# A fused attention and mixture-of-experts layer: expert work in steps of two 128-token tiles, x also passed turned, weights staged by single chunks

## The chip, the cores and the metric

The kernel runs on one core of one Trainium2 chip. Five engines have an instruction stream each: TensorE (PE; its weight loads are listed apart as PEld), VectorE (DVE), ScalarE (ACT), GpSimd (POOL) and SyncE (SP), which only issues DMA transfers. They meet at semaphores. A q behind an engine's name, as in PEldq or SPq, means the engine's own instruction queue: register work, waits and issues that keep no arithmetic unit busy. The metric is the device time of one execution in microseconds (us).

## The reference

8 batches of 512 tokens with 256 features go through linear attention with 16 heads and a gate, then through 16 experts, of which each token uses 4, and a shared expert.

```
q, k, v = heads(x @ Wq + bq), heads(x @ Wk + bk), heads(x @ Wv + bv)
q = elu(q) + 1;  k = elu(k) + 1
kv = einsum("bhsd,bhse->bhde", k, v);  attn = einsum("bhsd,bhde->bhse", q, kv)
x = layernorm(x + (sigmoid(x @ Wg + bg) * attn) @ Wo + bo)
scores = softmax(x @ gate_w.T)           # 16 experts in 4 groups
c = the scores of the 4 best experts inside the 2 best groups, else 0
a = silu(x @ w1[e]) * (x @ w3[e]);  y = sum_e c[:, e] * (a @ w2[e])
z = silu(x @ ws1) * (x @ ws3) @ ws2
out = layernorm(x + y + z)
```

Each expert has an inner width of 128, the shared one of 256.

## The kernel before

**Precision.** A large product is made of three 16-bit matmuls (`product`, lines 1147 to 1151): hi x hi, hi x lo, lo x hi. ScalarE makes the hi part of an operand (a copy to fp16), VectorE the lo part (the difference, bf16).

**Attention, 8 batches.** For batch b TensorE projects k and v of four token tiles, between them the output projection of batch b-1 (`project_out`), transposes x of batch b+1 (`transpose_x(x_in)`, line 1243), projects q, transposes the normalized x1 of batch b-1, projects the first half of the gate, sums k times v (`sum_kv`), projects the second half, counts and routes, and attends. x is loaded into `x_in`; its copy with the output bias is made on VectorE (`x_plus_bias`). VectorE's order in a batch: gate, routing of b-2, residual and norm statistics of b-1, lo parts of x, k, a weight split, q, lo parts of x1, kv, routing head. The reciprocal root of the norm is taken on GpSimd (`rstd_of`, four small operations), the normalization on ScalarE. The expert weights go to SBUF in nine stages of two chunks (an expert's w1, w3, w2 together are a chunk) and are split there (`split_hi`, `split_lo`). SyncE issues all loads in one hand-written order, with fills of zeros of 512 KB for rows of the sorted buffer that no token writes.

**Dispatch.** The batches form two waves of four. GpSimd scatters each token's x1 four times to a DRAM buffer sorted by expert (`expert_in`), 128 rows an instruction (line 440). Each expert has a region there. `plan_pairs` computes which expert and which row each pair has.

**Experts, 2 x 48 pairs.** A pair is 256 tokens of one expert: 16 tiles x 4 / 2 = 32 full pairs, and up to one partly filled for each of the 16 experts. For pair g:
- SyncE reads the row number from SBUF (`value_load`, line 327), waits for a free one of four token buffers, loads 256 rows (line 330) and stores the results of pair g-7 (line 334, `expert_out`).
- TensorE transposes the tokens of pair g+2 (`transpose_xs`), reads the number of the expert's weight chunk into a register (`chunk_of`, line 1345), makes four products of 256 columns (`up_pair`), and the down projection of pair g-2 (`down_pair`), six matmuls. Weight addresses hang on that register, so the queue computes them: two register instructions a product. `two_groups` is the body of a hardware loop over eight pairs; the first two of each turn read the chunk of pair g-2 again (line 1389).
- ScalarE: hi part of the transposed tokens, silu, results to SBUF, hi part of a. VectorE: lo part (1025), silu times h3 (line 1036), lo part of a (1044), and in some pairs a piece of the plan or, in wave 1, a `combine` of wave 0.

GpSimd gathers each token's four results (line 452) once a wave is stored, and VectorE adds them with their weights (1055).

**Tail.** The shared expert of batches 3 to 7, gathers and sums of wave 1, the final norms and stores.

The order of work is written out by hand on each engine; there is no scheduler.

## Time and profile before

| What | us |
|---|---|
| median of the runs (711.7 to 711.9) | 711.87 |
| the profiled execution | 707.36 |
| its span, first to last instruction | 705.5 |
| TensorE busy / VectorE / ScalarE / GpSimd | 527.1 / 427.4 / 300.1 / 290.1 |
| attention and first shared work, until the first token transposes | 266 |
| line 1036, first to last (96 pairs) | 273.8 to 588.8 |
| the rest | 117 |
| DMA: moved, mean rate | 118.6 MB, 168 GB/s |

The engines overlap, so the busy times are no sum. In the chain of work that ended last TensorE has 36% of the span, VectorE 19% and "issue" 15%: time in which an engine waited for nothing that the profile shows. SyncE's queue has 9%, and 6% is laid to another core or an unknown queue. The mean granted clock of TensorE is 0.916 of 2.4 GHz; it has only two levels, 2.4 and 1.2 GHz. A matmul's duration in the records is longer than its spacing, since matmuls are pipelined; the distance between two starts is what it costs. Of queue instructions the profile shows count, duration and the first and last start in a stretch.

### The profile page before, as it was taken

Reading aid. Unit: us, or ns where it says so; the run is one execution under the profiler, and the core shown is the slowest. Engines: PE = TensorE matmul, PEld = TensorE weight load, DVE = VectorE, ACT = ScalarE, POOL = GpSimd, SP = SyncE. Lnnn points to the kernel's source line nnn. Section 1 sums busy time; section 2 is a strip of 40 time slices with the busy share of each in tenths; the row PEclk is TensorE's granted clock in tenths of the full one; section 3 lists DMA queues with packets and bytes.
Section 4 is the critical chain, followed back from the end, with each engine's and each line's share of the span. In section 5 each row is a group of like instructions: output and inputs, shape, how many; then the busy total and the mean of one; then the engine's idle time right before and its main releaser. Section 6 shows DMA issues by size and latency. Waiting matters only on the chain.

```text
span 705.5 us, 13461 instructions
## 1 busy us (share of the span) xinstructions
PE 527.1 (75%) x3532; PEld 357.0 (51%) x3555; DVE 427.4 (61%) x1200; ACT 300.1 (43%) x659; POOL 290.1 (41%) x334
## 2 busy tenths in 40 slices
PE   1899887889897688789786688798888779665400
PEld 1355443555544357567574566576667566421300
DVE  2447783776864866666554444377757556652784
ACT  2536653436524343555454555356546445110100
POOL 1000126456446402454444200644446251777574
PEclk9999997899999899999999999899999989977755
DMA  7022428295451303767767766687787753333332
GB/s 202 13 75 76 156 90 284 82 304 209 177 185 68 103 18 106 239 204 230 232 228 259 238 223 216 180 235 233 211 261 231 223 181 134 105 120 89 94 114 99
DMA packets 64091, 118.63 MB, mean 168 GB/s; under 512 B 9760, under 2 KB 23088, under 8 KB 64048
## 3 DMA queue, kind: packets, MB, share of 16 engines
q1 hardware_dynamic: 51216, 84.55, 37.1%
q0 software_dynamic: 12288, 33.57, 15.1%
q8 instruction: 19, 0.31, 0.2%
q14 instruction: 24, 0.20, 0.1%
q10 hardware_dynamic: 544, 0.00, 0.0%
HBM read 55.17 MB, written 62.91 MB: 167 GB/s over the span
## 4 chain that ended last, share of the span: by engine, by line
PE 36%; DVE 19%; issue 15%; SPq 9%; another core or an unknown queue 6%; ACT 6%; DMA 5%; POOL 4%; ACTq 0%; DVEq 0%; POOLq 0%
PE t L1340 4%; PE h_even L1149 4%; PE h_even L1151 4%; PE h_odd L1149 3%; PE h_even L1150 3%; PE h_odd L1151 3%; PE h_odd L1150 3%; DVE x_all L1055 2%; SPq L327 2%; PE y L1186 2%; DMA kv<-expert_in 2%; SPq L330 1%; PE y L1373 1%; SPq L334 1%
## 5 line engine op out<-in xcount | busy, mean ns | idle before, releaser
L440 POOL DMA_INDIRECT expert_in<-x_all,slots x128 | 132.9, 1038 | 117.8 <-PE h_odd L1151 45.0
L452 POOL DMA_INDIRECT wa_stage<-expert_out,result_of x64 | 62.9, 983 | 35.3 <-issue 18.1
L1340 PE MATMUL t<-ident,kv 128*128 128x128 f32 x384 | 60.3, 280 | 19.4 <-DMA kv<-expert_in 15.0
L452 POOL DMA_INDIRECT q_fm<-expert_out,result_of x32 | 32.4, 1014 | 85.6 <-DMA expert_out<-q_exp 63.9
L426 POOL TENSOR_SCALAR neg_mean<-mv 128x4 f32<-128x4 f32 x16 | 4.6, 290 | 149.5 <-DVE mv L699 149.3
L1044 DVE TENSOR_TENSOR wa_lo<-bias_heads,wa_hi 128x256 bf16<-128x256 f32 x96 | 40.5, 422 | 41.3 <-ACT wa_hi L642 30.1
L1149 PE MATMUL h_even<-xsT_hi,we_hi 128*128 128x256 f16 x192 | 54.3, 283 | 10.7 <-issue 8.8
L1340 PEld LDWEIGHTS t<-ident,kv 128*128 128x128 f32 x384 | 45.3, 145 | 26.8 <-DMA kv<-expert_in 12.1
L1025 DVE TENSOR_TENSOR xsT_lo<-t,xsT_hi 128x512 bf16<-128x512 f32 x72 | 49.5, 688 | 11.6 <-ACT xsT_hi L617 5.9
L1150 PE MATMUL h_even<-xsT_lo,we_hi 128*128 128x256 bf16 x192 | 54.2, 282 | 2.5 <-issue 2.5
L1151 PE MATMUL h_even<-xsT_hi,we_lo 128*128 128x256 f16 x192 | 54.2, 282 | 1.4 <-issue 1.4
L617 ACT ACTIVATE xsT_hi<-t 128x512 f16<-128x512 f32 x72 | 42.0, 585 | 16.6 <-PE t L1340 12.8
L642 ACT ACTIVATE wa_hi<-bias_heads 128x256 f16<-128x256 f32 x96 | 39.7, 414 | 20.7 <-DVE bias_heads L1036 14.4
L1036 DVE TENSOR_TENSOR bias_heads<-h_odd,kv_heads 128x256 f32<-128x256 f32 x48 | 20.2, 420 | 41.8 <-ACT kv_heads L634 40.9
L1036 DVE TENSOR_TENSOR bias_heads<-h_even,kv_heads 128x256 f32<-128x256 f32 x48 | 20.1, 419 | 34.4 <-ACT kv_heads L634 30.9
L634 ACT ACTIVATE kv_heads<-h_odd 128x256 f32<-128x256 f32 x48 | 18.3, 381 | 52.8 <-remote 25.0
L1186 PE MATMUL y<-wo_sb,gated 128*128 128x256 f32 x128 | 33.3, 419 | 9.3 <-DVE gated L686 9.3
L452 POOL DMA_INDIRECT gate<-expert_out,result_of x32 | 30.5, 954 | 19.4 <-PE h_even L1151 10.0
L529 ACT ACTIVATE kv<-h_even 128x256 f32<-128x256 f32 x32 | 12.3, 386 | 58.3 <-PE h_even L1151 52.4
L634 ACT ACTIVATE kv_heads<-h_even 128x256 f32<-128x256 f32 x48 | 18.2, 380 | 43.8 <-PE h_even L1151 17.4
L1367 PE MATMUL y<-we_hi,wa_hi 128*128 x96 | 26.8, 279 | 12.6 <-issue 10.7
L624 ACT ACTIVATE k_exp<-y 128x512 f32<-128x512 f32 x48 | 28.7, 598 | 15.9 <-PE y L1373 14.3
(222 smaller groups left out, 1530.0 us busy)
## 6 DMA issues: line engine op xcount, KB each, us to landing
kv<-expert_in SPq DMA_DIRECT2D x96, 256.0 KB
expert_out<-k_exp SPq DMA_DIRECT2D x48, 256.0 KB
expert_out<-q_exp SPq DMA_DIRECT2D x48, 256.0 KB
expert_in<-wa_stage SPq DMA_DIRECT2D x16, 512.0 KB
expert_in<-wa_stage SPq DMA_DIRECT2D x32, 256.0 KB
stage<-in_L_ffn_w SPq DMA_DIRECT2D x48, 128.0 KB
x_in<-in_L_attn_x SPq DMA_DIRECT2D x8, 512.0 KB
out<-gated SPq DMA_DIRECT2D x8, 512.0 KB
```

The costliest lines, as they stand in the source:

```text
L440: pool.indirect_dma_start(xs_dram[b // WB], bass.IndirectOffsetOnAxis(ap=slots[:, b, t, j:j + 1], axis=0), x_all[:, b, t, :], None).then_i ...
L452: pool.indirect_dma_start(y_got[i][:, j, :], None, ys_dram[w], bass.IndirectOffsetOnAxis(ap=result_of[:, b, t, j:j + 1], axis=0)).then_inc ...
L617: act.activation(xsT_hi[r][:, :, :], t_bank[r % 2][:, :].rearrange("p (c n) -> p c n", c=KC), ACT.Copy).then_inc(xst_hi_ready, 1)
L642: act.activation(aT_hi[r % 2][:, :], a_pair, ACT.Copy).then_inc(at_hi_ready, 1)
L1025: dve.tensor_tensor(xsT_lo[r][:, :, :], t_bank[r % 2][:, :].rearrange("p (c n) -> p c n", c=KC), xsT_hi[r][:, :, :], ALU.subtract).then_in ...
L1036: dve.tensor_tensor(a_pair, h_banks[r % 2][0][:, 2 * P:], s_pair, ALU.mult).then_inc(pair_a_ready, 1)
L1044: dve.tensor_tensor(aT_lo[r % 2][:, :], a_pair, aT_hi[r % 2][:, :], ALU.subtract).then_inc(at_lo_ready, 1)
L1149: pe.matmul(dst, sta_hi, mov_hi, start=start, stop=False)
L1150: pe.matmul(dst, sta_hi, mov_lo, start=False, stop=False)
L1151: return pe.matmul(dst, sta_lo, mov_hi, start=False, stop=stop)
L1186: last = pe.matmul(y_bank[h][:, (t % 2) * D:(t % 2 + 1) * D], gated[:, c, t * P:(t + 1) * P], wo_sb[:, c, :], start=c == 0, stop=c == KC - 1)
L1340: last = pe.transpose(t_bank[r % 2][:, c * 2 * P + i * P:c * 2 * P + (i + 1) * P], xs[r][:, i, c * P:(c + 1) * P], ident[:, :])
```

## The change

**Steps of two tiles.** A region is cut in tiles of 128 tokens: 64 full ones and up to 16 partly filled, 80 a wave. A step takes tile p and tile p+40, in general of two experts. So there are 40 steps a wave instead of 48 pairs. SyncE reads two rows and issues two loads of 128 tokens. TensorE reads two chunk numbers and makes, in each half of the columns, four products of 128 columns; the down projection is one product for each tile. The transposes write their 128 columns with a step of two. Zero fills shrink to half.

```diff
-                row = sp.value_load(pair_row[0:1, NPAIR * w + p, :], min_val=0, max_val=SLOTS - PAIR)
+                rows = [sp.value_load(tile_row[0:1, h, NPAIR * w + p, :], min_val=0, max_val=SLOTS - P) for h in range(2)]
...
-                sp.dma_start(xs[r][:, :, :], rows_of(xs_dram[w], row)).then_inc(xs_loaded[r], 16)
+                for h in range(2):
+                    sp.dma_start(xs[r][h * P // 2:(h + 1) * P // 2, :, :],
+                                 rows_of(xs_dram[w], rows[h])).then_inc(xs_loaded[r], 16)
...
+            def chunks_of(g):
+                return [pe.value_load(tile_chunk[0:1, h, g, :], min_val=SHARED, max_val=NCH - 1) for h in range(2)]
...
+                for h, chunk in enumerate(chunks):
+                    tok = slice(h * P, (h + 1) * P)
+                    for k in range(2):
+                        for c in range(KC):
...
+                            last = product(h_banks[r % 2][0][:, k * PAIR + h * P:k * PAIR + (h + 1) * P],
+                                           we_hi[:, chunk, cols], we_lo[:, chunk, cols],
+                                           xsT_hi[r][:, c, tok], xsT_lo[r][:, c, tok], c == 0, c == KC - 1)
...
+                for h, chunk in enumerate(chunks):
+                    last = product(y_bank[r % 2][:, h * D:(h + 1) * D],
+                                   aT_hi[r % 2][:, h * P:(h + 1) * P], aT_lo[r % 2][:, h * P:(h + 1) * P],
+                                   we_hi[:, chunk, W13:], we_lo[:, chunk, W13:], True, True)
```

```order
L1340 MATMUL t<-ident,kv 128x128 x4
L1345 TENSOR_LOAD pair_chunk
L1345 ISA x2
L1149 ISA
L1149 MATMUL h_even<-xsT_hi,we_hi 128x256
L1150 MATMUL h_even<-xsT_lo,we_hi 128x256
L1151 REGISTER_ALU
L1151 MATMUL h_even<-xsT_hi,we_lo 128x256
```

and now:

```order
L1344 MATMUL t<-ident,kv 128x128 x4
L1348 ISA
L1348 TENSOR_LOAD tile_chunk
L1348 ISA x3
L1348 TENSOR_LOAD tile_chunk
L1348 ISA x2
L1165 ISA
L1165 MATMUL h_even<-xsT_hi,we_hi 128x128
L1166 MATMUL h_even<-xsT_lo,we_hi 128x128
L1167 REGISTER_ALU
L1167 MATMUL h_even<-xsT_hi,we_lo 128x128
```

The last five rows of each come four times in a row before, and eight times now, with half the columns. Then the down projection of the step two back: one ISA and one REGISTER_ALU before, two of each now. With the two or three instructions that wait, that is 17 register instructions a pair before and 31 a step now.

SyncE's queue in its first loop over wave 0, one load and one store. Before:

```order
L327 ISA
L327 TENSOR_LOAD pair_row
L327 ISA x2
L329 REGISTER_ALU
L330 ISA
L330 DMA kv<-expert_in 128x512
L333 REGISTER_ALU
L334 ISA
L334 DMA expert_out<-q_exp 128x512
```

and now:

```order
L331 TENSOR_LOAD tile_row
L331 ISA x3
L331 TENSOR_LOAD tile_row
L331 ISA x2
L333 REGISTER_ALU
L335 ISA
L335 DMA kv<-expert_in 64x512
L335 ISA
L335 DMA kv<-expert_in 64x512
L339 ISA
L340 ISA
L340 DMA expert_out<-k_exp 128x512
```

A second row number is read, and a second DMA issued, each of half the partitions.

**x turned.** The host passes x a second time with features outside; `load_xt` brings it to `x_in` as [128, 2, 512], and ScalarE and VectorE split it there. TensorE transposes x no more. x itself goes straight into `x_all`, where `x_plus_bias` adds the bias; x of batch 0 is issued behind the small loads and the first weight chunk. In TensorE's order the first half of the gate comes ahead of the transposes of x1, and the wait for the next batch's lo parts is at the batch's start.

```diff
-                if nxt:
-                    transpose_x(x_in, x_transposed)
...
                 project_features(b, 0, 2 * D, q_projected)
                 project_features(b, 1, 2 * D, q_projected)
-                if nxt:
-                    pe.wait_ge(xt_lo_ready, KC * (b + 2))
+                pe.wait_ge(q_exp_ready, KC * b + 1)
+                project_features(b, 0, 3 * D, g_projected)
...
                 if prev:
                     pe.wait_ge(x1_ready, b)
                     transpose_x(x_all[:, b - 1, :, :], x1_transposed)
-                pe.wait_ge(q_exp_ready, KC * b + 1)
-                project_features(b, 0, 3 * D, g_projected)
                 sum_kv(b)
```

**Weights by chunks.** Each of the 18 chunks is loaded, split and released alone, three a batch in batches 0 to 5: after the second k/v tile, between the gate's halves, and at the end (ScalarE); after k, after the lo parts of x1, and at the end (VectorE).

```diff
+            def load_chunk(c):
+                a1, a3, a2 = chunk_sources(c)
+                if c >= 2:
+                    sp.wait_ge(we_lo_ready, c - 1)
...
+            for b in range(1, 6):
+                next_x(b + 1)
+                load_chunk(3 * b + 1)
+                load_chunk(3 * b + 2)
+                if b > 1:
+                    for i in range(2 * (b - 2), 2 * (b - 1)):
+                        fill_spare(i)
+                if b < 5:
+                    load_chunk(3 * b + 3)
```

**Plan and norms.** `plan_tiles` has nine steps on rows of 80 tiles (eight on 48 pairs before) and for wave 0 stands behind the last residual instead of ahead of the shared expert's first product. `place_results` has a step more, for the two halves. Variance plus epsilon, and where it is used the negated mean, are computed on VectorE in `norm_moments`; GpSimd keeps the power and, but for the last five norms, the product. In wave 1 the final norms of batches 0 to 2 go from VectorE to ScalarE (`final_norm`, in a step each tile from step 17 on), and the combines are spread evenly over the 40 steps.

```diff
             def rstd_of(ln):
                 pool.wait_ge(mv_ready, ln + 1)
-                pool.tensor_scalar(neg_mean[:, :], mv[:, :, 0], -1.0, None, ALU.mult)
-                pool.tensor_tensor(var_eps[:, :], mv[:, :, 1], eps[:, :], ALU.add).then_inc(rstd_step, 1)
...
+                power = pool.tensor_tensor(rstd[:, :], var_eps[:, :], minus_half[:, :], ALU.pow)
```

## Rows read from the trace of the kernel before

**Rows 1.** Three stages: us, busy us and instructions of each engine, granted clock, DMA, GB/s
```profile
0.00:266.00 266.00, 214.23 (x1174) 123.08 (x1194) 168.75 (x538) 120.02 (x255) 90.79 (x114) 0.94 0.41 135
266.00:589.00 323.00, 262.20 (x2114) 207.68 (x2112) 191.56 (x492) 166.36 (x380) 127.34 (x136) 0.96 0.69 217
589.00:705.50 116.50, 50.71 (x248) 26.22 (x250) 67.12 (x172) 13.69 (x24) 71.96 (x84) 0.73 0.34 107
```
**Rows 2.** Line 1036, a pair's h3*silu on VectorE: durations (ns), first to last start (us)
```profile
L1036 DVE TENSOR_TENSOR bias_heads<-h_even,kv_heads x48: 402/420/426, 273.8 to 586.8; 128x256 f32<-128x256 f32 x48
L1036 DVE TENSOR_TENSOR bias_heads<-h_odd,kv_heads x48: 403/424/426, 275.8 to 588.8; 128x256 f32<-128x256 f32 x48
```
**Rows 3.** Who waited for whom, 266 to 589 us: total us, times, longest
```profile
PEld h_even L1149 <- issue: 19.8, 38, 1.3
...
PEld y L1367 <- issue: 18.4, 24, 1.3
...
PE t L1340 <- DMA kv<-expert_in: 15.0, 11, 3.8
...
PEld t L1340 <- DMA kv<-expert_in: 12.1, 7, 4.0
```
**Rows 4.** TensorE's own queue, lines 1345, 1149, 1151: count, durations (ns), starts
```profile
L1345 PEldq TENSOR_LOAD <-pair_chunk x5: 298/302/605, 466.5 to 476.0; - x5
...
L1345 PEldq TENSOR_LOAD <-pair_chunk x1: 302/302/302, 564.4 to 564.4; - x1
...
L1149 PEldq FUSED_REGOPS  x4: 46/46/46, 565.0 to 565.8; - x4
...
L1151 PEldq ALU_OP  x4: 32/32/32, 565.2 to 565.9; - x4
```
**Rows 5.** TensorE in order of time: start us, us, line, matmul
```profile
563.06 0.60 PE L1340 MATMUL t<-ident,kv 128*128 128x128 f32 x4
563.50 0.27 PE L1149 MATMUL h_even<-xsT_hi,we_hi 128*128 128x256 f16 x1
563.61 0.27 PE L1150 MATMUL h_even<-xsT_lo,we_hi 128*128 128x256 bf16 x1
...
565.46 0.60 PE L1340 MATMUL t<-ident,kv 128*128 128x128 f32 x4
```
**Rows 6.** SyncE's DMA issues in order of time, a fast and a slow stretch
```profile
562.65 0.35 SPq L330 DMA_DIRECT2D kv<-expert_in  x1
563.88 0.33 SPq L334 DMA_DIRECT2D expert_out<-k_exp  x1
...
338.60 0.73 SPq L330 DMA_DIRECT2D kv<-expert_in  x1
340.11 0.01 SPq L334 DMA_DIRECT2D expert_out<-q_exp  x1
342.38 0.71 SPq L330 DMA_DIRECT2D kv<-expert_in  x1
```
**Rows 7.** Who waited for whom, 0 to 266 us
```profile
ACT we_hi L516 <- DMA stage<-in_L_ffn_w: 31.8, 7, 7.4
...
DVE logits L730 <- remote: 19.8, 5, 8.9
...
PE t L1156 <- ACT x_all L510: 17.6, 7, 5.8
...
PEld t L1156 <- ACT x_all L510: 10.9, 2, 6.3
```
**Rows 8.** The start in order of time: last small load, x plus bias
```profile
6.63 0.42 SPq L281 DMA_DIRECT2D plan_sb<-in_plan_consts  x1
...
14.49 1.22 DVE L704 TENSOR_TENSOR x_all<-x_in,b_o 128x1024 f32<-128x1024 f32 x1 [6.29 <-DMA plan_sb<-in_plan_consts]
```
**Rows 9.** GpSimd in order of time, the last normalization
```profile
699.16 0.23 POOL L426 TENSOR_SCALAR neg_mean<-mv 128x4 f32<-128x4 f32 x1 [4.34 <-DVE mv L699]
...
700.74 0.20 POOL L431 TENSOR_TENSOR shift<-neg_mean,rstd 128x4 f32<-128x4 f32 x1
```

More of the change, by code:

```diff
@@ L17 @@
 P = 128
-PLAN_STEPS = 8
+PLAN_STEPS = 9
 LN_EPS = 1e-5
@@ L654, in _ @@
             group(1)
-            with act.Fori(1, all_groups // 2 - 1) as q2:
+            with act.Fori(1, GROUPS_OF_PAIRS // 2) as q2:
                 group(2 * q2)
                 group(2 * q2 + 1)
-            group(all_groups - 2)
-            group(all_groups - 1, last=True)
+            for p in range(NPAIR):
+                pair(NPAIR + p, p % RING, GROUPS_OF_PAIRS + p // RING, p < NPAIR - 2)
+                b, t = (p - NORM_PAIR) // 9, (p - NORM_PAIR) % 9
+                if 0 <= b < EARLY and t < TT:
+                    final_norm(b, t)
             for r in range(2, RING):
@@ L1008, in _ @@
             residual(NB - 1, True)
+            for part in range(PLAN_STEPS):
+                plan_tiles(0, part)
             shared_hidden(1)
@@ L1026, in xst_lo, with pair @@
                                   xsT_hi[r][:, :, :], ALU.subtract).then_inc(xst_lo_ready, 1)
-            def pair(g, r, ahead=True, add=None, norm=None, whole=True, part=None):
+            def pair(g, r, ahead=True, add=(), part=None):
                 if ahead:
@@ L1073, in final_norm, with group @@
                     last.then_inc(out_ready, 1)
-            def group(q, b=None, tiles=(), norm=None, whole=True, parts=(), last=False):
+            def group(q, parts=()):
                 for r in range(RING):
-                    add = [(b, i // TOP_K, i % TOP_K) for i in tiles[r]] if tiles else None
-                    pair(RING * q + r, r, not (last and r >= 2), add, norm, whole,
-                         parts[r] if r < len(parts) else None)
-            q1 = GROUPS_OF_PAIRS
+                    pair(RING * q + r, r, part=parts[r] if r < len(parts) else None)
             xst_lo(0, 0)
```

417 lines of the change are left out of this document (198 added, 219 removed).

## Prediction, made before the changed kernel was run

> **What bounds the kernel now.** I read the three stages first. Attention takes 266 us with TensorE busy 214 of them, the expert pairs take 323 us with TensorE busy 262, and the tail takes 116.5 us with TensorE at 51 [rows 1] (busy columns in the order TensorE, its weight loads, VectorE, ScalarE, GpSimd). The pair stage is the one that the change rebuilds. Line 1036 runs once for each of the 96 pairs, from 273.8 to 588.8 us: 315 us, 3.28 us a pair [rows 2]. What ends last there? The list of waits names no engine. The two largest idle times that I quote are "issue", 19.8 and 18.4 us, which is time in which nothing in the profile holds TensorE back, and after them the loads of gathered tokens, 15.0 + 12.1 us [rows 3].
>
> "Issue" becomes plain in TensorE's own instruction queue. In a clean stretch five loads of the expert's chunk number (line 1345) start from 466.5 to 476.0: 2.38 us a pair [rows 4]. The array would need nearly the same: its transposes start 2.40 us apart, each 256-column matmul 0.11 us after the one before [rows 5]. So the queue and the array are level at 2.4 us, and any register work put into the queue shows in the time. Its prices: the chunk load starts at 564.4 and the first address computation of the pair follows at 565.0, with the instruction ahead of the load some 0.7 us. Each product of three matmuls needs two register instructions, one for the hi and one for the lo address (lines 1149 and 1151). Their four starts lie 0.8 and 0.7 us apart, over three products 0.24 us each [rows 4]. The three matmuls themselves are not what takes that: the array needs 0.33 us for them and has them waiting.
>
> **Pairs.** The change cuts the padding: 80 pair steps of two tiles instead of 96 of 256 tokens. Each step, though, now serves two experts. Queue of TensorE, clean, per step: 2.38 as before; + 0.7 for a second chunk load; + 4 x 0.24 = 0.96 because the up projection is eight products of 128 columns instead of four of 256; + 0.24 for a second pair of addresses in the down projection. That is 4.28 us. Two steps of every eight load their older chunks again (the pair of the previous loop turn): 2 x 0.7 x 1/4 = 0.35, against 0.18 before. So 4.63 us against 2.56. Over all: 80 x 4.63 = 370 us against 96 x 2.56 = 245.
>
> The array is no longer level with it. Transposes 4 x 0.11 and down matmuls 6 x 0.11 stay, 1.1 us [rows 5]. No row shows a 128-column matmul, so 24 of them cost between half of the 256-column spacing, 1.3 us, and all of it, 2.6. That is 2.4 to 3.7 us, below 4.63 at either end. I take 2.4.
>
> The Trainium skill (TensorE: Matmul & The Clock Gate, section "Wait — 56ns, not 53.3ns?") gives about 56 ns between starts at 128 columns with the full clock; by that the 24 are 1.34 us and the array would again need 2.4. No run here shows it yet.
>
> The measured 315 us hold 70 more than the clean 245. The token loads are 27 of them [rows 3]; with a step twice as long they land in time, and I let them go. The other 43, 0.45 us a pair, are short slow spells of the queue. Per step they stay, 80 x 0.45 = 36. Bounds: nothing (370 in all), or in proportion to register instructions, which go from 17 to 31 a step, 0.82 us and 65 (435). I take 406: it keeps the rate that was measured. **The pair stage costs 406 - 315 = +91 us**, 55 to 120.
>
> **SyncE** gets a second row number and a second load per step. In a fast stretch load to store is 1.23 us, of which 0.35 is the issue; in a slow one two loads lie 3.78 us apart [rows 6]. Added are a value load, some 0.7 as on TensorE, and an issue, 0.35 to 0.5. It would need 3 us in fast and some 6 in slow stretches. Four token buffers let it run ahead, so I cost it at nothing; the cover is TensorE's 4.63. VectorE and ScalarE keep their instructions per step and do 80 instead of 96. Their wave-0 combines and norms lie under the queue.
>
> **Attention.** (a) x comes turned, so eight transposes a batch (0.87 us) leave TensorE, and the gate's first half, six matmuls of 512 columns at twice 0.11, 1.3 us, is moved ahead of the transposes of x1. TensorE waits there for the normalization, 17.6 + 10.9 us in nine waits [rows 7]. A batch gains between 0 and 2.2 us; I take 1.2 for six batches, -7. (b) Weights by single chunks: ScalarE waited 31.8 us for stage loads, and VectorE 19.8 for nothing the profile names, 8.9 of it once, in the batch behind a burst of four zero fills [rows 7]. Half the fills go and the weights come in smaller pieces. I take -7, most of that one stall, between 0 and -12. (c) The two small operations of the norm go from GpSimd to VectorE, -2 over eight batches, and the plan moves behind the last residual, -2 with its longer rows counted. (d) The start: x(0) for the residual is issued behind one chunk, about 3.5 us after the last small load (6.63). VectorE's x plus bias, now at 14.49 [rows 8], waits for it, and the split of the first weights stands behind that in its queue, with TensorE behind it. Between 0 and +6, taken +3. **Sum -15**, 0 to -25.
>
> **Tail.** It is a row of gathers on GpSimd and a last norm. Negation to last product is 699.16 to 700.74 [rows 9]; only the power is left of it, so some 0.7 us goes at the end and as much in each of three norms between gathers. -3, 0 to -5.
>
> **Sum.** Span 705.5 - 15 + 91 - 3 = 778.5. The profiled execution was 1.9 us longer than its span, and the median of the runs 4.5 us above that execution: 784.9, so **785 us**.
>
> **Rivals.** First, the forecast's mechanism is absent: register instructions go beside the work and a step costs what a pair does, 3.28 us. Then 80 x 3.28 = 262, -53, and the median is 641. For it: before, array and queue are level, so the trace alone can't tell which one set 2.4. Against it: the four register starts stand 0.24 us apart where the array takes 0.33 for a product, so these are the queue's own spacings. It decides if a step takes under 4.2 us; 0.08 for all that ends faster than before. Second, SyncE becomes the bound: if its slow spells took half the time, a step is (4.63 + 6.3) / 2 = 5.5 us, 437 us, median 816; if all of it, 504 us and 883. For it: a slow stretch before had nothing but longer instructions; against: four buffers ahead. Third, the clock. The granted clock was 0.96 in this stage [rows 1], with an array that was nearly always busy; now it is busy about half. At 1.2 GHz the 2.4 us become 4.8, still about the queue's pace: 80 x (4.8 + 0.45) = 420, median 799. If the queue can't run ahead over its chunk loads, 4.8 + 1.4 = 6.2 us, 496 us and 875.
>
> Beside it the Trainium skill (TensorE: Matmul & The Clock Gate, "HAM oscillation — how this bites in real kernels") tells of kernels whose pauses bring the half clock; the trace agrees as far as half-clock stretches here follow waits. It is the third rival, not a term.
>
> **How the numbers follow.** Forecast case, 740 to 830: 0.78. Above 830: 0.10, SyncE taking over 0.04 and the clock 0.06; what they cost below that lies in the forecast's range. Between 713 and 740 (most slow spells gone and attention at its best): 0.03. No change: 0.01. Faster: 0.08. The ends are the bounds of the terms: 705.5 - 25 + 55 - 5 + 6.4 = 737 and 705.5 + 0 + 120 + 0 + 6.4 = 832, nearly. A measurement of this kernel tells 0.2%, 1.4 us, from no change.
>
> **What would show it.** Chunk loads on TensorE's queue in twos, steps of 4.3 to 5.3 us from first to last line-1036 operation (now under another number), 390 to 430 us in all; idle time of the array laid to "issue", several times today's; fewer waits for token loads. The four register spacings stay at 0.24 us. Attend of the last batch some 10 to 15 us earlier. It would be wrong if a step took under 4.2 us, or if 128-column matmuls stood 0.11 us apart at the full clock and the array, not its queue, set the pace.

## The result, and the profile after

| What | before | after |
|---|---|---|
| median of the runs, us | 711.79 (709.4 to 711.9) | 812.79 (810.6 to 815.2) |
| the profiled execution, us | 707.36 | 813.95 |
| its span, us | 705.5 | 812.2 |

The changed kernel is slower: ratio 1.143, 95% interval 1.139 to 1.147. The forecast was 785 us, 740 to 830, slower with 0.91. Every ratio here and below compares the means of a kernel's faster executions, those within 1.5% of its fastest, so it can differ a little from the quotient of two medians.

Three stages of the kernel after, cut where line 1066 (line 1036 before) takes over, in the columns of [rows 1]:

```profile
0.00:284.00 284.00, 209.65 (x1116) 117.21 (x1135) 174.26 (x569) 120.32 (x255) 89.20 (x97) 0.92 0.38 119
284.00:693.00 409.00, 292.34 (x2716) 221.15 (x2715) 172.46 (x436) 146.52 (x328) 124.89 (x130) 0.89 0.46 146
693.00:812.20 119.20, 52.79 (x249) 26.65 (x251) 67.05 (x175) 13.43 (x24) 69.15 (x69) 0.69 0.32 104
```

Line 1066, a step's h3 times silu on VectorE, to be held against [rows 2]:

```profile
L1066 DVE TENSOR_TENSOR bias_heads<-h_even,kv_heads x40: 414/425/426, 291.8 to 688.7; 128x256 f32<-128x256 f32 x40
L1066 DVE TENSOR_TENSOR bias_heads<-h_odd,kv_heads x40: 414/424/425, 295.2 to 692.7; 128x256 f32<-128x256 f32 x40
```

It runs from 291.8 to 692.7 us: 401 us in place of 315, 5.07 us a step in place of 3.28 a pair. It also begins 18 us later, and what follows takes 119.5 us in place of 116.7. So the pair stage is 86 of the 107 us of span, the time ahead of it 18, the tail 3.

Who waited for whom in that stage, to be held against [rows 3]:

```profile
ACT kv_heads L653 <- remote: 84.3, 20, 10.0
...
PEld h_even L1165 <- issue: 51.2, 43, 2.6
PEld h_odd L1165 <- issue: 45.7, 40, 2.5
...
PEld y L1165 <- issue: 38.4, 67, 2.6
...
PEld t L1344 <- DMA kv<-expert_in: 1.8, 3, 0.8
```

TensorE's weight loads now lose 135 us to "issue" in the three rows shown; before, the same three rows came to 54 (19.8, 18.4 and 15.8). The waits for token loads, 27 us before, are 2.8 (this row and 1.0 us of the matmuls'). And there is a row that I had not looked for: ScalarE's silu, `kv_heads` at line 653, waits 84.3 us for "remote", a releaser that the profile can't name. The trace of before has the same row, and it is the largest idle time that any row there lays to "issue" or "remote"; I had left it out of [rows 3]:

```profile
ACT kv_heads L634 <- remote: 36.5, 13, 6.5
```

It is taken up below.

TensorE's own queue in a clean stretch, to be held against [rows 4]: three chunk loads, and the low-part address computations of one step:

```profile
L1348 PEldq TENSOR_LOAD <-tile_chunk x3: 303/306/313, 473.4 to 478.4; - x3
...
L1167 PEldq ALU_OP  x8: 32/32/32, 480.0 to 481.7; - x8
```

The array in the same step and at the start of the next, in order of time, to be held against [rows 5]:

```profile
479.97 0.23 PE L1165 MATMUL h_even<-xsT_hi,we_hi 128*128 128x128 f16 x1 [0.99 <-issue]
480.04 0.22 PE L1166 MATMUL h_even<-xsT_lo,we_hi 128*128 128x128 bf16 x1
480.09 0.22 PE L1167 MATMUL h_even<-xsT_hi,we_lo 128*128 128x128 f16 x1
480.21 0.23 PE L1165 MATMUL h_even<-xsT_hi,we_hi 128*128 128x128 f16 x1
...
484.25 0.23 PE L1165 MATMUL h_odd<-wa_hi,we_hi 128*128 128x128 f16 x1 [0.97 <-issue]
```

The eight low-part address computations of a step stand between 480.0 and 481.7, 0.24 us apart, as before. The three matmuls of a product start at 479.97, 480.04 and 480.09, the next product at 480.21: the array has done three matmuls of 128 columns in 0.18 us and stands idle until the queue has its next address. The first product of the next step starts at 484.25. A clean step is 4.28 us.

The Trainium skill (TensorE: Matmul & The Clock Gate, section "Wait — 56ns, not 53.3ns?") gives about 56 ns between such starts at the full clock. The trace agrees: 0.05 to 0.07 us, with a granted clock of 1.00 from 473 to 482 us.

### The profile page after: what moved, and what is told of

Same layout as the page of the kernel before. It is cut to its first block, busy times and chain, and to the rows that moved or that the text cites. A ratio compares the mean times of both kernels' runs of the same rounds, so it can differ in the third digit from the quotient of the medians.

```text
span 812.2 us, 15300 instructions
## 1 busy us (share of the span) xinstructions
PE 554.8 (68%) x4077; PEld 365.0 (45%) x4099; DVE 413.8 (51%) x1178; ACT 280.3 (35%) x607; POOL 283.2 (35%) x296
## 4 chain that ended last, share of the span: by engine, by line
PE 36%; issue 16%; DVE 15%; another core or an unknown queue 13%; SPq 7%; ACT 6%; POOL 4%; DMA 2%; DVEq 1%; POOLq 0%; ACTq 0%
PE h_even L1165 5%; PE h_odd L1165 4%; PE h_even L1167 3%; PE y L1202 3%; PE h_even L1166 3%; PE t L1344 3%; PE h_odd L1167 2%; PE y L1165 2%; PE h_odd L1166 2%; SPq L331 2%; SPq L335 2%; PE y L1166 2%; DVE x_all L1083 2%; ACT x_all L519 2%
## 5 line engine op out<-in xcount | busy, mean ns | idle before, releaser
L1165 PE MATMUL h_even<-xsT_hi,we_hi 128*128 128x128 f16 x320 | 77.0, 242 | 41.0 <-issue 33.4
L1165 PE MATMUL y<-we_hi,wa_hi 128*128 (+1 forms) x192 | 58.4, 304 | 37.9 <-issue 33.7
L458 POOL DMA_INDIRECT wa_stage<-expert_out,result_of x64 | 63.1, 985 | 46.5 <-issue 16.1
L1167 PE MATMUL h_even<-xsT_hi,we_lo 128*128 128x128 f16 x320 | 75.0, 235 | 1.8 <-issue 1.6
L1166 PE MATMUL h_even<-xsT_lo,we_hi 128*128 128x128 bf16 x320 | 75.2, 236 | 0.0
L431 POOL TENSOR_TENSOR rstd<-var_eps,minus_half 128x4 f32<-128x4 f32 x16 | 18.4, 1147 | 150.3 <-DVE var_eps L726 150.2
L1165 PEld LDWEIGHTS h_even<-xsT_hi,we_hi 128*128 x320 | 32.8, 102 | 63.8 <-issue 51.2
L1166 PE MATMUL y<-we_lo,wa_hi 128*128 (+1 forms) x192 | 57.9, 302 | 1.4 <-issue 1.2
L1167 PE MATMUL y<-we_hi,wa_lo 128*128 (+1 forms) x192 | 57.5, 299 | 0.0
L1165 PE MATMUL h_odd<-xsT_hi,we_hi 128*128 128x128 f16 x160 | 42.5, 268 | 16.1 <-issue 10.8
L1165 PE MATMUL h_odd<-wa_hi,we_hi 128*128 128x128 f16 x160 | 37.3, 234 | 19.8 <-issue 11.8
L1344 PEld LDWEIGHTS t<-ident,kv 128*128 128x128 f32 x320 | 40.5, 154 | 15.5 <-issue 10.3
```

The lines of the kernel that those rows point to most:

```text
L431: power = pool.tensor_tensor(rstd[:, :], var_eps[:, :], minus_half[:, :], ALU.pow)
L458: pool.indirect_dma_start(y_got[i][:, j, :], None, ys_dram[w], bass.IndirectOffsetOnAxis(ap=result_of[:, b, t, j:j + 1], axis=0)).then_inc ...
L1165: pe.matmul(dst, sta_hi, mov_hi, start=start, stop=False)
L1166: pe.matmul(dst, sta_hi, mov_lo, start=False, stop=False)
L1167: return pe.matmul(dst, sta_lo, mov_hi, start=False, stop=stop)
L1344: last = pe.transpose(turned[:, :, i], xs[r][:, i, c * P:(c + 1) * P], ident[:, :])
```

## Experiments

Each kernel was timed beside the kernel before on the same chip. The kernel before itself took 709.5 us in the first group (e1 to e4), 701.5 in the second (e5 to e8), 701.2 in the third (e9 to e11) and 647.6 in the fourth (e12), so ratios to it are compared, and stages by line 1036 or 1066 of each profile (1067 in e8_plan_back). A stage's length is read from one profiled execution for each kernel, while the executions of one kernel lie 3 to 17 us apart; a difference of a few us between two stages is therefore no more than a sign. The expectations count from 813 and 712 us. In a group where the kernel before is quicker, the measured ratio times 712 is the number to hold against them.

### Is it TensorE's queue? Its register work taken away and added

**e1_static**: no chunk load and no address computation is left in a step; of register instructions only the two or three that wait remain.

```diff
-            def chunks_of(g):
-                return [pe.value_load(tile_chunk[0:1, h, g, :], ...) for h in range(2)]
+            def chunks_of(i):
+                return [SHARED + (2 * i + h) % E for h in range(2)]
```

> The changed kernel, with the two chunk numbers of a step fixed when the program is built (experts 0 to 15 in turn) in place of the two chunk loads, so that no product computes an address. Most tiles then use the wrong expert's weights; all else, the number of matmuls too, stays. Queue theory (TensorE's own instruction queue sets the step, 5.07 us now): 1.44 us of chunk loads and the 0.24 us spacing of ten products go, the step falls to what comes next, the array (2.4 us) or SyncE (3 us), and the pair stage from 401 us to between 240 and 300; the whole run about 660 to 710 us. Array theory (matmuls, or their clock, set the step): pair stage above 370 us, run above 780. SyncE theory (row numbers and issues set it): above 370 us too.

Measured: 749.9 us, ratio 1.059 (1.050 to 1.068). Pair stage:

```profile
L1066 DVE TENSOR_TENSOR bias_heads<-h_even,kv_heads x40: 408/425/426, 286.1 to 627.4; 128x256 f32<-128x256 f32 x40
L1066 DVE TENSOR_TENSOR bias_heads<-h_odd,kv_heads x40: 414/425/426, 288.3 to 629.1; 128x256 f32<-128x256 f32 x40
```

343 us: 58 less, but not the 240 to 300 of the queue theory, and a run of 749.9 us where that had 660 to 710. Its direction holds and the array theory falls (the array's work and its count are the same), yet something else holds the step well above 3 us.

**e2_one_load**: one chunk load a step, `2 * [pe.value_load(tile_chunk[0:1, 0, g, :], ...)]`.

> The changed kernel, with one chunk load a step on TensorE in place of two; both tiles of a step use the first one's expert, so the second tile gets the wrong weights. The address instructions of the products stay. Queue theory: 0.72 us less for each of the 100 sets of loads (80 steps and 20 reloads), 72 us less, pair stage 329 us, run 741. SyncE or array theory: within 5 us of the changed kernel, 813.

Measured: 762.3 us, ratio 1.071 (1.064 to 1.079), pair stage from 289.8 to 644.1 us, 354 us. That is 47 us of the stage where the queue theory had 72 (and a run of 741).

**e3_before_two_loads**: the same test from the other side.

```diff
             def chunk_of(g):
+                pe.value_load(pair_chunk[0:1, g, :], min_val=SHARED, max_val=NCH - 1)
                 return pe.value_load(pair_chunk[0:1, g, :], min_val=SHARED, max_val=NCH - 1)
```

> The kernel before, with each chunk load on TensorE made twice (the second result is used). Queue theory: 120 further loads (96 pairs and 24 reloads) of 0.72 us, 86 us more, run 798, if the queue sets the pace all the time; at least half of that, 755, if waits for tokens cover a part. Rival (array and queue stand level and the queue runs ahead over a load): under 20 us more.

Measured: 748.6 us, ratio 1.052 (1.041 to 1.062), pair stage 278.3 to 629.1 us, 351 in place of 315. Of 86 us that were added to the queue, 36 show. That is between the two theories: the queue sets the pace in part of the stage; in the rest another thing makes the pairs late, and queue work hides in it.

**e4_one_row**: SyncE reads one row number a step, `rows = 2 * [sp.value_load(tile_row[0:1, 0, ...])]`.

> The changed kernel, with one row number read a step on SyncE in place of two; both loads of a step fetch the first tile's rows, so the second tile of each step is not computed. SyncE's queue is shorter by about 0.75 us a step, its DMAs stay. Queue theory (TensorE's queue sets the step, SyncE runs ahead): within 5 us of 813. SyncE theory (it sets the step at least in slow stretches): 30 to 60 us less, 753 to 783.

Measured: 799.0 us, ratio 1.120 (1.109 to 1.130), pair stage 284.1 to 677.0 us, 393 in place of 401. The total fell by more than that, 2.0% against the changed kernel's ratio, because this profile's pair stage also began 8 us sooner, behind smaller standstills in attention; the expectation of the queue theory (within 5 us) is missed by that. SyncE is not the bound of the changed kernel: 0.75 us a step less on its queue bring 0.1 us a step, and TensorE waits 2.8 us in all for token loads there. Whether those 8 us are real, one profile of each can't tell.

### What holds the other steps: runs of indirect transfers

The steps' lengths in e1_static gave the hint: with no register work left, many steps of 2.0 to 2.5 us had one of 5 to 6.3 behind them, and the changed kernel has 6.2 to 6.5 us every second step too. Every second step is when GpSimd scatters: `pool.wait_ge(h_ready, 2 * i)`, then four transfers. One such step of the changed kernel in order of time, GpSimd first:

```profile
383.15 0.95 POOL L446 DMA_INDIRECT expert_in<-x_all,slots  x1 [5.16 <-PE h_odd L1167]
...
386.93 0.96 POOL L446 DMA_INDIRECT expert_in<-x_all,slots  x1 [0.30 <-issue]
```

VectorE's line 1066 in the same stretch:

```profile
383.33 0.42 DVE L1066 TENSOR_TENSOR bias_heads<-h_odd,kv_heads 128x256 f32<-128x256 f32 x1 [1.34 <-ACT kv_heads L653]
...
389.56 0.42 DVE L1066 TENSOR_TENSOR bias_heads<-h_even,kv_heads 128x256 f32<-128x256 f32 x1 [3.71 <-ACT kv_heads L653]
```

And TensorE at the end of that step:

```profile
387.74 0.27 PE L1167 MATMUL y<-we_hi,wa_lo 128*128 x1
388.99 0.63 PE L1344 MATMUL t<-ident,kv 128*128 128x128 f32 x4 [0.98 <-issue]
```

The scatters start 1.26 us apart. TensorE's last matmul of the step starts at 387.74, the next thing it does at 388.99, 1.1 us behind the last scatter's end; VectorE goes on at 389.56. In between TensorE's and SyncE's queues move in lockstep, one or two register instructions each 0.7 us, where an instruction otherwise takes 0.05. The "short slow spells" of my prediction, the slow stretch of [rows 6] and the unnamed 8.9 us of [rows 7] look alike. Theory R: toward the end of a run of indirect transfers and for 1 to 2 us behind it the other engines' queues nearly stand still, and a longer run stops them longer. (The longest pauses behind a run that are quoted below are 2.3 and 2.4 us.)

**e5_spread**: the same transfers, spread.

```diff
-            for i in range(WT):
+            for i in range(2 * WT):
                 if i > 0:
-                    pool.wait_ge(h_ready, 2 * i)
-                dispatch(rows[first + TOP_K * i:first + TOP_K * (i + 1)])
+                    pool.wait_ge(h_ready, i)
+                dispatch(rows[first + 2 * i:first + 2 * (i + 1)])
...
-                    pool.wait_ge(h_ready, NPAIR + 9 * k // 4)
...
                 for j in range(TOP_K):
+                    if 0 < k < WT:
+                        pool.wait_ge(h_ready, NPAIR + 9 * (TOP_K * k + j) // 16)
```

> The changed kernel, with GpSimd's indirect transfers in the pair stage spread: the 64 scatters of wave 0's steps in twos, one step apart, where they went in fours every second step, and the 64 gathers of wave 1's steps one by one, 9/16 of a step apart, where they went in fours. Their number and data are the same. Theory R (every engine stands still toward the end of a run of indirect transfers and for 1 to 2 us behind it, and a longer run stops them longer): the steps of 6.2 to 6.5 us go, the mean step falls from 5.07 to about 4.6, the run from 813 to between 770 and 795. Rival (what a transfer costs the others does not depend on the run it is in, or the long steps have another cause): within 5 us of 813.

Measured: 778.8 us, ratio 1.110 (1.101 to 1.118), so 2.9% less than the changed kernel's 1.143; times 712 that is 790 us, inside the 770 to 795 expected. Its pair stage:

```profile
L1066 DVE TENSOR_TENSOR bias_heads<-h_even,kv_heads x40: 414/424/426, 287.2 to 660.4; 128x256 f32<-128x256 f32 x40
L1066 DVE TENSOR_TENSOR bias_heads<-h_odd,kv_heads x40: 423/424/426, 290.6 to 664.4; 128x256 f32<-128x256 f32 x40
```

Its wait for "remote" in that stage:

```profile
ACT kv_heads L653 <- remote: 9.5, 1, 9.5
```

377 us, 24 less, 4.72 us a step where I had 4.6. "Remote" falls from 84.3 us in 20 waits to 9.5 in one. Steps of 6 us and more are left only where old chunks are loaded again and at the change of waves; most of the rest take 3.9 to 5.2. The one at the change of waves takes 11.7 us, from 489.0 to 500.7, and the only wait for "remote" ends in it. The edit had left one run there, eight gathers one behind the other:

```profile
488.50 0.99 POOL L458 DMA_INDIRECT q_fm<-expert_out,result_of  x1 [59.69 <-DMA expert_out<-q_exp]
...
497.30 0.94 POOL L458 DMA_INDIRECT gate<-expert_out,result_of  x1 [0.30 <-issue]
```

The changed kernel was not timed in this group, so the 24 us also hold the difference between two groups. e8_plan_back, further down, was, and has the runs of four:

```profile
L1067 DVE TENSOR_TENSOR bias_heads<-h_even,kv_heads x40: 416/425/428, 279.4 to 666.4; 128x256 f32<-128x256 f32 x40
L1067 DVE TENSOR_TENSOR bias_heads<-h_odd,kv_heads x40: 411/425/426, 282.5 to 670.3; 128x256 f32<-128x256 f32 x40
```

That is 391 us, with 81.7 us of "remote" at silu. Against it e5_spread's stage is 14 us shorter.

**e6_bunch**: the other way, runs of eight, `pool.wait_ge(h_ready, 4 * i)` and `2 * TOP_K` scatters each.

> The changed kernel, with the scatters of wave 0's steps in runs of eight, four steps apart, in place of four, two steps apart. Theory R: each run stops the other engines longer than two runs of four do (a run of 12 stopped VectorE for 10 us in the attention, a run of four for some 2): wave 0's steps take 10 to 40 us more, the run 823 to 853. Rival (cost per transfer fixed): within 5 us of 813. If bunching is cheaper, theory R is wrong in its dependence on length.

Measured: 815.3 us, ratio 1.164 (1.155 to 1.173); times 712 that is 829 us, where 823 to 853 were expected. A step with a run in it, GpSimd in order of time:

```profile
339.99 0.96 POOL L446 DMA_INDIRECT expert_in<-x_all,slots  x1 [15.37 <-PE h_odd L1167]
...
348.85 0.96 POOL L446 DMA_INDIRECT expert_in<-x_all,slots  x1 [0.30 <-issue]
```

Line 1066 around it:

```profile
340.16 0.42 DVE L1066 TENSOR_TENSOR bias_heads<-h_odd,kv_heads 128x256 f32<-128x256 f32 x1 [0.81 <-ACT kv_heads L653]
...
352.20 0.42 DVE L1066 TENSOR_TENSOR bias_heads<-h_even,kv_heads 128x256 f32<-128x256 f32 x1 [9.48 <-ACT kv_heads L653]
```

The eight scatters end at 349.8, and the step takes 12.04 us. Seven steps of wave 0 are like it. Wave 0's steps together take 212 us in place of 195, 17 more, and silu's "remote" grows from 84.3 to 119.5 us. Runs of two, four and eight give steps of 4.3, 6.3 and 12.0 us. Part of that is given back: the step behind a long one is often short, 2.0 to 4.2 us. What the runs cost shows in wave 0 as a whole, by the three kernels of this group: 184 us with twos (e5_spread), 189 with fours (e8_plan_back), 212 with eights, for the same 64 scatters. So a fixed cost per transfer is refuted, and the step from two to four costs far less than the one from four to eight.

**e9_before_spread**: the same edit in the kernel before, one transfer at a time (in the trace they still come in ones, twos and threes, seldom four, and seven and eight gathers at two places).

> The kernel before, with GpSimd's indirect transfers in the pair stage spread: the 64 scatters of wave 0's pairs one by one, 5/8 of a pair apart, where they went in fours every two and a half pairs, and wave 1's 64 gathers one by one where they went in fours. Theory R (a run of indirect transfers holds up the instruction queues of the other engines from its fourth transfer on, until it is over): the 70 us that the pair stage has above 96 clean pairs fall by half or more, so 25 to 45 us less, 0.94 to 0.965 of the time before. Rival (those 70 us are waits for token loads and for single slow instructions, whatever GpSimd does): within 5 us of before.

Measured: 677.3 us beside 701.2, ratio 0.971 (0.959 to 0.983): faster than before, by 24 us of the medians and 20 by the ratio. The interval excludes no change, but it reaches from 1.7 to 4.1%.

```profile
L1037 DVE TENSOR_TENSOR bias_heads<-h_even,kv_heads x48: 402/425/426, 274.5 to 563.8; 128x256 f32<-128x256 f32 x48
L1037 DVE TENSOR_TENSOR bias_heads<-h_odd,kv_heads x48: 402/425/426, 276.5 to 565.5; 128x256 f32<-128x256 f32 x48
```

Its wait for "remote" in that stage:

```profile
ACT kv_heads L635 <- remote: 12.0, 3, 5.1
```

The pair stage is 291 us in place of 315, silu's wait for "remote" 12.0 us where the trace of before has 36.5. The gain is under the 25 to 45 expected; the rival's "within 5 us" falls. (The profile with 315 and 36.5 us is from a group in which this kernel is 10 us slower, so the stages alone would not settle it; the times of one group do.)

**e11_static_spread**: both limits off, the edits of e1_static and e5_spread.

> The changed kernel with fixed chunk numbers as in e1_static (most tiles use the wrong expert's weights) and the pair stage's transfers spread as in e5_spread. Queue theory together with theory R: both limits of a step are gone and the array (2.4 us) or SyncE (3 us) is left, pair stage 215 to 270 us where e1_static had 343 and e5_spread 377; about 0.87 to 0.95 of the kernel before. If a step still takes over 4 us, a third limit stands behind those two.

Measured: 725.1 us beside 701.2, ratio 1.037 (1.028 to 1.047), pair stage 322 us. Both miss what I expected, 0.87 to 0.95 and 215 to 270 us. A third limit stands behind the two, and the waits of the stage name it:

```profile
PE t L1344 <- DMA kv<-expert_in: 82.3, 60, 3.2
...
PEld t L1344 <- DMA kv<-expert_in: 39.2, 21, 3.3
```

SyncE's issues there, in order of time:

```profile
502.31 1.16 SPq L335 DMA_DIRECT2D kv<-expert_in  x2
503.67 0.43 SPq L340 DMA_DIRECT2D expert_out<-q_exp  x1
506.03 1.16 SPq L335 DMA_DIRECT2D kv<-expert_in  x2
```

And in the part of wave 0 where each step also fills rows with zeros (line 307):

```profile
380.96 1.18 SPq L335 DMA_DIRECT2D kv<-expert_in  x2
383.01 0.52 SPq L307 DMA_DIRECT2D expert_in<-wa_stage  x1
...
386.15 1.17 SPq L335 DMA_DIRECT2D kv<-expert_in  x2
```

TensorE waits for token loads, 82.3 + 39.2 us, while SyncE itself waits for almost nothing. SyncE gets its two loads out every 3.7 us: two issues take 1.16 us, a store 0.43, and reading two row numbers some 1.5 of the rest. Other such distances in wave 1 are 3.2 to 4.4 us. In the sixteen steps with a fill, for which a third row number is read and a third transfer issued, they are 5.0 to 5.8 us. So with TensorE's queue free a step would cost 3.2 to 5.8 us by SyncE's, not the array's 2.4. My expectation named it with 3 us and was too low; steps of two tiles fill both queues.

### Attention and plan

**e7_attention**: the kernel before with x turned, single chunks, the new order of the gate and the norm's small operations; pairs, fills and plan as before.

```diff
-            load_stage(0)
+            load_chunk(0)
+            load_x(0)
+            load_chunk(1)
...
-            batch(0, False, False, True, early=0)
...
+            for b in range(NB):
+                batch(b, b > 0, b > 1, b < NB - 1, plan=b == WB + 1)
```

> The kernel before with the change of its attention alone: x also turned, weights by single chunks, the gate's order, the two small operations of the norm on VectorE. The pairs of 256 tokens, the plan and its place, the fills and the final norms are those of before. My forecast's step (attention worth -15 us, less the plan's -2): about 699. What the trace of after suggests (2 us gained in each undisturbed batch, +3 at the start, the rest given back in standstills behind scatters): 705 to 717.

Measured: 701.8 us beside 701.5, ratio 1.004 (0.999 to 1.009): no change. Times 712 that is 715 us: the 705 to 717 of the second reading hold, my forecast's 699 doesn't. VectorE's wait for "remote" at the routing head in this kernel:

```profile
DVE logits L735 <- remote: 29.0, 5, 10.3
```

And in the changed kernel:

```profile
DVE logits L755 <- remote: 31.9, 5, 10.8
```

29.0 and 31.9 us where [rows 7] has 19.8. The largest of these in the changed kernel:

```profile
238.89 0.29 DVE L755 TENSOR_REDUCE logits<-t 128x64 f32<-128x128 f32 x1 [10.83 <-remote]
```

GpSimd in the same stretch:

```profile
226.74 0.96 POOL L446 DMA_INDIRECT expert_in<-x_all,slots  x1 [0.30 <-issue]
...
235.60 0.96 POOL L446 DMA_INDIRECT expert_in<-x_all,slots  x1 [0.30 <-issue]
```

TensorE's routing matmuls, which line 755 reads, are done at 228.8 us. VectorE goes on at 238.9, 2.3 us behind the end of a run of 13 scatters. Before, the same scatters came as a run of six and one of seven with 1.4 us between them, and line 730 had waited 2.0 us. The quicker batch seems to let GpSimd pass its next wait without a pause, so that two runs become one; e7_attention has the same run of 13 and a wait of 10.3 us.

**e10_best**: e7_attention, e9_before_spread, and in attention five groups of two or three scatters, each behind a step of TensorE, in place of four of three.

> The kernel before with the change of its attention (as in e7_attention), the pair stage's transfers spread as in e9_before_spread, and the attention's twelve scatters a batch in five groups of two or three, each behind a step of TensorE, where they went in threes that joined into runs of six to thirteen. Theory R: the standstills of VectorE in the attention (10.8, 9.9, 5.1 and 3.7 us in the changed kernel) go too, 15 to 30 us, and the attention change shows its 2 us a batch: 40 to 70 us below the kernel before, 0.90 to 0.945. Rival for the attention part (VectorE stands still for another reason): the same as e9_before_spread.

Measured: 677.4 us beside 701.2, ratio 0.968 (0.955 to 0.980), the same as e9_before_spread (one of its executions, at 2790 us, is left out). The groups did not stay apart: twelve scatters of 1.27 us take 15 of a batch's 24 us, GpSimd falls behind, and its waits are already met when it comes to them. Runs of 8 to 12 are still there, with 20.5 us of "remote" at the routing head. So the edit did not do what it was to do, and for the attention half this run decides nothing; the 0.90 to 0.945 expected are missed.

**e12_landed**: e9_before_spread, and in attention a wait after every third scatter until all have landed.

```diff
+                    n = TOP_K * k + j
+                    if 0 < n < WT * TOP_K and n % 3 == 0:
+                        pool.wait_ge(dispatched[(n - 1) // (TT * TOP_K)], 16 * ((n - 1) % (TT * TOP_K) + 1))
```

> The kernel of e9_before_spread, with one edit more: in the attention GpSimd waits after every third scatter until all scatters so far have landed, so that no run there is longer than three (there: 12, 9, 9, 6, 6, 7). Theory R (standstills belong to runs of four and more): VectorE's gap of 10.4 us at 110.6 us and ScalarE's of 7.0 and 5.9 us shrink to under 3 us, and the attention ends 5 to 20 us earlier, unless the pauses make GpSimd late for the normalizations; run 0.94 to 0.97 of the kernel before. Rival (what counts is the number of transfers in a stretch of time, or the zero fills and loads beside them): the gaps stay and the run is as e9_before_spread, 0.97, or slower.

Measured: 665.1 us, but the kernel before took 647.6 beside it, ratio 1.021 (1.016 to 1.027): slower, where 0.94 to 0.97 were expected. The profiled execution took 668.7 us, the longest of its six.

```profile
POOL expert_in L443 <- DMA expert_in<-x_all,slots: 53.1, 17, 7.3
PE t L1160 <- ACT x_all L514: 43.8, 6, 16.0
ACT x_all L514 <- POOL shift L431: 34.5, 6, 13.6
```

Runs are of three, and no wait for "remote" is left at the routing head. GpSimd pays for it with 53 us of waiting and comes late to the norms: TensorE waits 43.8 us for normalized rows where it waited 14.8. The last attend starts at 237.1 us, 226.4 in e9_before_spread. How much the pauses save can't be told here: in this group the kernel before takes 647.6 us, and this profile has no "remote" row anywhere, not in the tail either, where GpSimd's gathers come sixteen in a row as before. In e9_before_spread's tail, with such runs, VectorE and ScalarE wait 20 us for "remote". The pair stage, which has the edit of e9_before_spread and nothing more, takes 271.5 us where that took 291.0. So here the pauses had little to save and show their cost alone, and theory R is not tested in the attention. Runs of these lengths do not bring standstills at all times. What differed is open: this group and the one of e9 to e11 carry the same chip number, 9, and lie minutes apart, yet the kernel before took 701.2 us in one and 647.6 in the other. That the missing standstills are what makes it 54 us quicker fits, but was not tested, and no profile of the kernel before was taken in this group.

**e8_plan_back**: the changed kernel with `plan_tiles(0, part)` ahead of `shared_hidden(0)` again.

> The changed kernel, with the plan of wave 0 ahead of the shared expert's first product on VectorE, as in the kernel before, in place of behind the last residual. My forecast's step (moving it behind the residual gains 2 us): 815. What the trace of after suggests (the last normalization and with it the transposes of x1 wait 8 us for VectorE there, and the pair stage begins later by that): 803 to 807.

Measured: 795.1 us, ratio 1.135 (1.127 to 1.144); the changed kernel's interval, 1.139 to 1.147, touches it, so the time alone doesn't settle it. Times 712 it is 808 us, just above the 803 to 807 of the second reading and below my forecast's 815. In the profile the way from the last attend to the first line-1066 operation is 60.8 us, against 64.6 and 64.0 in e5_spread and e6_bunch, which ran on the same chip with the plan behind the residual. The last wait at the routing head is 11.7 us in all three. By these the place costs 3 to 4 us: not the gain of 2 of my forecast, and half of the 8 that I then read from the trace. It is one profile of each; e1_static and e11_static_spread, with the plan behind the residual in other groups and 1 us less of that wait, have 61.2 and 61.5 us, so the cost may be less.

## Why the prediction was right, and where it was not

**The pair stage, +91 forecast, +86 measured.** The clean step, 4.28 us, was worked out from [rows 4] and is 4.28, to a hundredth by luck, since its prices were read to a tenth. Its parts held: a chunk load, two register instructions a product at 0.24 us, the array below the queue. e2_one_load and e3_before_two_loads move with the count of register instructions, which the array does not explain. The first rival (register work beside the matmuls, 641 us) is refuted. The token loads went, as the sum said.

**The term of 0.45 us a step** was near in size (401 less 80 clean steps and their reloads, 370, is 31 us; I had 36) and wrong in kind, so that it came near was luck. I called these spells short slow spells of the queue and let them go on per step. e5_spread, e6_bunch and e9_before_spread show that they hang on runs of GpSimd's transfers: 24 us of them go when the runs are broken up (14 against e8_plan_back of the same group), and wave 0 gets 17 more when they are doubled (23 against e8_plan_back). It may have come out near since 64 scatters and 64 gathers stand beside the stage in both kernels. I had the lockstep of both queues in view in [rows 6] and did not set GpSimd's rows beside it; nor had I shown silu's 36.5 us of "remote", which stood in the same list of waits.

**Queue and other limits.** My sum took every queue instruction at its full price. e3_before_two_loads shows 36 of 86 us, e2_one_load 47 of 72. For this change it held since the queue is above the rest, 4.6 against SyncE's 3.7. That margin isn't there in the sixteen steps with a fill, where SyncE needs 5.0 us and more; there the four buffers ahead seem to cover it, since TensorE waits 2.8 us in all for tokens. Starting from a kernel where limits stand level, a price per instruction is an upper end.

**SyncE** (second rival): e4_one_row moves the stage by 8 us, so it is not the bound. Its own step is 3.2 to 4.4 us in e11_static_spread's wave 1, above the 3 that I worked out for fast stretches, and 5.0 to 5.8 with a fill, which my sum for SyncE left out. **The clock** (third rival): the granted clock in the stage is 0.89 after 0.96, and the queue's spacing is the same; it brought neither 420 nor 496 us.

**Attention and start, -15 forecast, +18 measured**, is the step that failed: its range was 0 to -25, and I had the last attend 10 to 15 us earlier.
- (d) the start: +3 forecast; the first attend is at 41.0 us in place of 37.6, +3.4.
- (a), (c) per batch: undisturbed batches take 24.0 us (from 63.9 to 88.0 to 112.2) where the kernel before takes 26.1 and 26.4. That gain is real, 2 us and more a batch.
- (b) I counted 8.9 us of standstill as gone because half the fills go. They don't decide it; runs of scatters do, as far as e7_attention and the rows of 226 to 239 us show it. The wait for "remote" at the routing head rose from 19.8 to 31.9 us, and e7_attention, which keeps all the fills, has 29.0. The gain per batch is given back: the last attend is at 228.7 in place of 225.5.
- The first line-1066 operation comes behind the last attend 63.1 us later, in place of 48.3. Of these 14.8 some 8.3 are the last standstill (10.2 us against 1.9), the plan's longer rows 2.5 (8.3 us against 5.8), its place 3 to 4. From 248.9 to 267.1 us VectorE pauses once, for 0.7 us, so what is put on it there shows. I had counted the move as a gain.

The plan on VectorE, behind the last residual; the operation behind it, line 1014, is what ScalarE and then the last normalization wait for:

```profile
250.91 0.42 DVE L852 TENSOR_TENSOR stage<-total,plan_sb 128x256 f32<-128x256 f32 x1
...
258.95 0.23 DVE L886 SCALAR_TENSOR_TENSOR tile_row<-plan_sb,stage 1x80 int32<-1x80 f32 x1
259.11 0.67 DVE L1014 TENSOR_TENSOR x_in<-h_odd,x_in 128x512 f32<-128x512 f32 x1
```

ScalarE there:

```profile
259.81 0.63 ACT L611 ACTIVATE a_hi<-x_in 128x512 f16<-128x512 f32 x1 [9.74 <-DVE x_in L1014]
```

**Tail, -3 forecast, +2.8 measured.** The norm after the last gather lost its small operations, but the tail is one long run of gathers. In the experiments that leave the changed kernel's tail alone it took 112.9 to 120.3 us, and 108.4 to 115.4 in those on the kernel before; a term of 3 us can't be read in that. What the profile shows of it is "remote" again: 42 us on VectorE and ScalarE after, 33 before.

**The sum.** 785 against 812.8: attention and start 33 too low, the tail 6 too low, the pair stage 5 too high, and the step from span to median (+6.4 forecast, +0.6 here) 6 too high. The total fell in the range because the largest term was right and two others erred the other way by 11 us; the range of the attention term (0 to -25) did not hold its value, nor did the tail's (0 to -5).

## What to carry to other kernels

Count what an engine's instruction queue must do per unit of work, register loads and address computations, beside what the array must do: a matmul of 256 columns made as two of 128 leaves the array's work as it was and doubles the queue's. Less padding (80 steps of 256 rows in place of 96) is worth nothing if each step then pays for two dynamic addresses. And look at GpSimd's row when other engines wait for nothing that has a name: break runs of indirect transfers into ones and twos where its time allows. That alone made the kernel before 2.9% faster (e9_before_spread, 1.7 to 4.1%). It and e10_best, which holds the same edit, are the only versions here that beat both kernels beyond their intervals. It was measured where the kernel before takes 701 us; where it takes 648 and no standstill shows, there may be nothing to gain.

## What the runs showed of the hardware that I had not expected

- A run of indirect transfers from GpSimd, 1.27 us each, slows the other engines' queues to one or two instructions each 0.7 us. A step around a run of two, four and eight took 4.3, 6.3 and 12.0 us, wave 0 with its 64 transfers 184, 189 and 212 us; in attention runs of 12 and 13 stopped VectorE for 9.9 and 10.8 us. In e12_landed's profile runs of sixteen brought no such stop. All of TensorE, VectorE, ScalarE and SyncE are held, matmuls that are already queued aside.
- The Trainium skill (SBUF — State Buffer, section "SBUF: two separate sides") says that of the engines' ports only the pair shared by VectorE and GpSimd is contended and that TensorE and ScalarE never wait there. The measurement goes beyond that: ScalarE's silu and TensorE's and SyncE's queues are held as well, so the shared pair alone can't be the cause. What is shared here the runs don't tell. The DMA engines are no candidate by their share alone: it was 0.18 to 0.36 in each 2 us of the stop from 229 to 239 us. Nor are loads of instructions: the DMA queues show none from 383 to 391 us, around the stop at 389.
- The same kernel took 701 to 712 us on four occasions and 647.6 on a fifth, and the one profile from that fifth, of e12_landed, shows no such stop. Two of the five, with 701.2 and 647.6 us, carry the same chip number, so it is not shown that the chip makes the difference. A ratio within one group is worth more than a time, and what a remedy brings has to be measured where it is to run.
